# A feature-interaction tower on one core: contractions joined and moved, the split of the next chunk ahead of its border, and one tile of seven of the first chunk as one f32 product

## The reference, cut to what matters

```python
e = jnp.stack([tbl_f[ids[:, f]] for f in range(39)], axis=1)        # B=512, M=39, D=16
x0 = xk = e
for W in (W0, W1):                                                 # H = 128 and 128
    Wr = W.reshape(39, xk.shape[1], 128)
    xk = jnp.einsum('bid,bjd,ijh->bhd', x0, xk, Wr)
    outs.append(xk)
z = jnp.sum(jnp.concatenate(outs, axis=1), axis=-1)                # (512, 256)
h = jnp.concatenate([z, dense_ctx], axis=1)
h = jnp.maximum(h @ W_top1 + b_top1, 0.0)
h = jnp.maximum(h @ W_top2 + b_top2, 0.0)
y = h @ W_top3                                                     # (512, 1)
```

## Time and profile before

| what | us |
|---|---|
| runs, median of 3 | 365.79 |
| the profiled execution | 365.56 |
| its span in the profile | 363.8 |
| TensorE (matmul) busy | 229.9 (63%) |
| VectorE busy | 164.8 (45%) |
| ScalarE busy | 158.9 (44%) |
| GpSimd busy | 98.0 (27%) |

### The profile page before, as it was taken

One profiled execution on the slowest core, in us unless ns is written; L12 is line 12 of the kernel. 1 busy time (PEld: TensorE's weight loads), 2 busy tenths in 40 slices (PEclk: granted clock), 3 DMA queues, 4 the chain that ended last, 5 costly groups with the idle time before them and its releaser, 6 DMA issues.

```text
span 363.8 us, 4707 instructions
## 1 busy us (share of the span) xinstructions
PE 229.9 (63%) x1673; PEld 176.2 (48%) x1673; DVE 164.8 (45%) x333; ACT 158.9 (44%) x307; POOL 98.0 (27%) x107
## 2 busy tenths in 40 slices
PE   5311100010001001889998999989999999999997
PEld 4200000000000000746765887667688877788896
DVE  4440000000000100589897867979784867745411
ACT  4600000000000300488887757986856877666411
POOL 5777777777777730000000000000000000000000
PEclk9655555555555555699999999999999999999999
DMA  6800100000000000019100000000000000000000
GB/s 175 253 14 6 10 6 6 7 7 6 6 7 6 6 5 0 0 31 304 46 21 2 1 2 1 2 0 3 1 2 2 0 3 0 3 0 2 0 2 0
DMA packets 7834, 8.61 MB, mean 24 GB/s; under 512 B 2759, under 2 KB 5420, under 8 KB 7812
## 3 DMA queue, kind: packets, MB, share of 16 engines
q1 hardware_dynamic: 4516, 7.48, 7.2%
q0 software_dynamic: 3296, 0.85, 2.5%
HBM read 8.32 MB, written 0.00 MB: 23 GB/s over the span
## 4 chain that ended last, share of the span: by engine, by line
PE 48%; issue 35%; DVE 7%; ACT 7%; another core or an unknown queue 2%; DMA 1%; ACTq 0%; DVEq 0%
PE turn_bank L542 10%; PE g_bank L512 5%; PE pair_bank L455 5%; PE x_bank L479 5%; PE x_bank L482 4%; PE x_bank L481 4%; DVE onehot L791 3%; ACT prod_hi L1027 2%; DVE prod_lo L864 2%; PE x_bank L522 2%; PE turn_bank L580 2%; PE g_bank L706 2%; PE turn_bank L553 1%; ACT prod L1022 1%
## 5 line engine op out<-in xcount | busy, mean ns | idle before, releaser
L430 POOL DMA_INDIRECT emb<-tbl,ids_sb x103 | 97.8, 950 | 33.5 <-issue 31.1
L1022 ACT ACTIVATE prod<-pair_bank 128x512 f32<-128x512 f32 (+1 forms) x112 | 66.2, 600 | 43.0 <-PE pair_bank L455 38.7
L864 DVE TENSOR_TENSOR prod_lo<-prod,prod_hi 128x512 fp32r<-128x512 f32 x96 | 65.1, 686 | 2.6
L479 PE MATMUL x_bank<-prod_hi,pair_w_hi 128*128 128x512 f32 (+1 forms) x112 | 63.4, 566 | 2.0 <-DVE prod_lo L864 1.9
L1142 ACT ACTIVATE looked<-pair_bank 128x192 f32<-128x192 f32 x2 | 0.6, 328 | 104.4 <-remote 104.4
L808 DVE COPY_PREDICATED looked<-odd,pair_bank 128x192 f32<-128x192 int32 x2 | 0.6, 370 | 97.6 <-issue 97.6
L455 PE MATMUL pair_bank<-x,sel 117*128 117x512 bf16 (+1 forms) x112 | 42.8, 384 | 0.9 <-ACT x L1004 0.7
L542 PE MATMUL turn_bank<-g_sb,w_sb 128*128 128x128 f32 x312 | 42.3, 279 | 0.0
L542 PEld LDWEIGHTS turn_bank<-g_sb,w_sb 128*128 128x128 f32 x312 | 39.4, 192 | 3.0 <-issue 1.2
L1027 ACT ACTIVATE prod_hi<-prod 128x512 fp32r<-128x512 f32 x64 | 40.0, 625 | 0.1
L482 PE MATMUL x_bank<-prod_hi,pair_w_lo 128*128 128x512 f32 x96 | 38.1, 397 | 0.0
(11 more groups left out here) (143 smaller groups left out, 315.2 us busy)
## 6 DMA issues: line engine op xcount, KB each, us to landing
emb<-tbl,ids_sb POOLq DMA_INDIRECT x103
tab<-small SPq DMA_DIRECT2D x2, 560.0 KB
wt<-w_top SPq DMA_DIRECT2D x2, 512.0 KB, 4.4
tab<-small SPq DMA_DIRECT2D x1, 504.0 KB
wa<-pair_w_a SPq DMA_DIRECT2D x1, 448.0 KB
wb<-pair_w_b SPq DMA_DIRECT2D x1, 448.0 KB
wtd<-w_dense SPq DMA_DIRECT2D x1, 256.0 KB
dense_sb<-dense_t SPq DMA_DIRECT2D x1, 256.0 KB
```

The source lines that it names most:

```text
L430: pool.indirect_dma_start(out=emb[:, at:at + D], out_offset=None, in_=tables[f], in_offset=bass.IndirectOffsetOnAxis(ap=ids_sb[:, c * M + ...
L479: mm = pe.matmul(x1_banks[k % 2][:, :], pair_w_hi[p, t, :], hi(n), start=(t == 0), stop=(t == FULL))
L864: dve.tensor_tensor(lo(n), prod[rows, n % RING, :], prod_hi[rows, n % RING2, :], ALU.subtract).then_inc(lo_done, 1)
L1022: act.activation(prod[0:ROWS[t], n % RING, :], pair_bank[n % 2][0:ROWS[t], :], ACT.Square).then_inc(sq_done, 1)
```

## The change

- `contract_d(k, 0)` and `(k, 1)` stand together in one step (`G_AT = 4`), at the second tile of the block after next. The second half's G goes to free columns of `misc_bank` and of `x1_banks[k % 2]`. The four copies follow one step later (`G_KEPT = 2`). `turn_x` moves from a block's first tile to its fifth, `spread_x` from the third to the sixth.
- `look_up_later` runs as one piece of twenty products at a block's fifth tile, into the two G banks; its copies and picks become two of half the size. Chunks 2 and 3 are looked up one block later. The second part of the ids is spread at tile 17 instead of 10, and `later_ids` holds 24 slots, of which the first 4 are used twice.
- The seam goes; all borders have one form. The next chunk's splits stand at tiles 1, 2 and 6 of block 3 for chunk 1, and at tiles 0, 1, 3 and 4 for chunks 2 and 3. The turns and the copies to `x3` stand at the end of block 3's last step, ahead of two tiles of layer 1. Chunk 0's layer 2 runs in blocks 2 and 3 of chunk 1 like the others.
- Tile 3 of each of the four blocks of chunk 0 (`whole(n)`) is neither rounded nor subtracted: ScalarE squares it into free columns of `emb`, and layer 1 takes it as one f32 product with an f32 weight tile.
- `keep_x1h` on ScalarE stands between the square and the rounding of its step.

```diff
+WHOLE_AT = 3
...
-SEAMS = (1,)
-SPLIT_AT = (4, 6)
+SPLIT_AT = ((), ((1, 2), (6, 6)), ((0, 1), (3, 4)), ((0, 1), (3, 4)))
...
-G_AT = (3, 6)
+G_AT = 4
+G_KEPT = 2
+XT_AT = 4
+SPREAD_AT = 5
...
-LATE_AT = (NT + 1, NT + 3)
+LATE_AT = (NT + 1, 2 * NT + 3)
+IDS_HELD = 24
+LOOK_AT = 4
...
+        prod_whole = emb[:, 0:COLS]
...
+        def look_step(c, part):
+            return ((c - 1) * NB + part + (c > 1 and PARTS[c] < 3)) * NT + LOOK_AT
+        def look_at(n):
...
+        def hot_at(n):
+            return [(c, part, r) for c in range(1, NCH) for part in range(PARTS[c]) for r in range(HOT)
+                    if max(look_step(c, part) - 6 + r, (c - 1) * NB * NT) == n]
...
+        def later_cols(f):
+            return g_bank[f // 2][:, f % 2 * 2 * E:(f % 2 + 1) * 2 * E]
+        def later_rows(half, row):
+            return looked_rows(g_bank[half], 2, row)
...
+        def whole(n):
+            return n < NB * NT and n % NT == WHOLE_AT
+        def split_tiles(n):
+            return n - sum(whole(m) for m in range(n))
...
+            if pair == 1:
+                return x1_banks[k % 2][:, 0:2 * QC] if half else misc_bank[:, QC:3 * QC]
...
+                kept = 2 * (c * NB - 2)
+                if c and part == 0:
+                    pe.wait_ge(g_dve, kept)
+                if c and part == 1:
+                    pe.wait_ge(g_act, kept)
...
+                wait(pe, g_act, 2 * (k - 1))
...
-                pe.wait_ge(lo_done, n + 1)
+                if whole(n):
+                    pe.wait_ge(sq_done, n + 1)
+                    pe.matmul(x1_banks[k % 2][:, :], pair_w_whole[:, :], prod_whole, start=False,
+                              stop=False).then_inc(l1_done, 1)
+                    return
+                pe.wait_ge(lo_done, split_tiles(n + 1))
                 if t == 0:
                     wait(pe, x1_done, k - 1)
+                    wait(pe, g_dve, 2 * (k - 1))
                     if k == 1:
                         pe.wait_ge(dense_act, 2)
-                    c, j = divmod(k, NB)
...
+                if k == K - 1:
+                    pe.wait_ge(g_dve, 2 * k)
...
-                    pe.wait_ge(xblk_done, k + 1)
-                if k == K - 1 and pair == 1:
+                    pe.wait_ge(xblk_done, min(k + 2, K))
+                    pe.wait_ge(picked, len(SETS) + looks_ahead_of((k + 2) * NT))
+                    wait(pe, g_act, 2 * k)
+                    wait(pe, g_dve, 2 * k)
+                elif k == K - 1:
                     pe.wait_ge(x1_done, K + 1)
-                else:
-                    wait(pe, g_act, 2 * k + pair)
-                    wait(pe, g_dve, 2 * k + pair)
...
-            def look_up_later(c, part, r0, r1):
-                for r in range(r0, r1):
+            def look_up_later(c, part):
+                pe.wait_ge(picked, len(SETS) + nth(c, part))
+                pe.wait_ge(dense_dve, 2)
+                k = look_step(c, part) // NT
+                kept = 2 * (k - 1)
+                wait(pe, g_act, kept)
+                wait(pe, g_dve, kept)
+                for r in range(HOT):
                     pe.wait_ge(later_hot_done, HOT * nth(c, part) + r + 1)
                     for f in range(LATER):
                         rows = tab_parts[part // 2][:, LATER * (part % 2) + f, 2 * r:2 * r + 2, :, :]
-                        mm = pe.matmul(later_bank(part)[:, f * 2 * E:(f + 1) * 2 * E], later_hot[:, r, f, :],
-                                       rows.rearrange("p r q d -> p (r q d)"), start=(r == 0 and f == 0),
-                                       stop=(r == HOT - 1 and f == LATER - 1))
+                        mm = pe.matmul(later_cols(f), later_hot[:, r, f, :],
+                                       rows.rearrange("p r q d -> p (r q d)"), start=(r == 0 and f % 2 == 0),
+                                       stop=(r == HOT - 1 and f % 2 == 1))
                     mm.then_inc(later_row, 1)
...
-            def seam(c):
...
                 if late and t == 0:
                     layer1(m)
                     layer1(m + 1)
-                    pe.wait_ge(x1_done, n // NT - 1)
-                    turn(c, 0)
-                    pe.wait_ge(xblk_done, n // NT)
-                    turn(c, 1)
-                    pe.wait_ge(sq_done, n - 1)
-                    turn(c, 2)
-                    layer1(m + 2)
                 if n < TILES:
                     select_pair(n)
                 if m >= 0 and (not late or t >= LAG1):
                     layer1(m)
-                if late and t == 1:
-                    layer1(m + 2)
-                if t == 0 and n < TILES:
+                if late and t in (1, 2):
+                    layer1(m + 1)
+                if c + 1 < NCH and j == NB - 1 and t == NT - 1:
+                    pe.wait_ge(x1_done, n // NT)
+                    turn(c + 1, 0)
+                    pe.wait_ge(xblk_done, n // NT + 1)
+                    turn(c + 1, 1)
+                    pe.wait_ge(sq_done, n)
+                    turn(c + 1, 2)
+                if t == XT_AT and n < TILES:
                     turn_x(n // NT)
-                if u == 0 and k >= 1 and not ended(k - 1):
+                for part in look_at(n):
+                    look_up_later(*part)
+                if u == 0 and k >= 1:
                     turn_x1(k - 1)
-                if u in G_AT and k >= 1 and not ended(k - 1):
-                    contract_d(k - 1, G_AT.index(u))
+                if u == G_AT and k >= 1:
+                    contract_d(k - 1, 0)
+                    contract_d(k - 1, 1)
                 if n >= TILES:
                     return
...
             def take_lo(n):
+                if whole(n):
+                    return
                 k, t = divmod(n, NT)
                 if t in DVE_ROUNDS:
-                    dve.wait_ge(hi_dve, len(DVE_ROUNDS) * k + DVE_TO[t + 1])
+                    dve.wait_ge(hi_dve, len(DVE_ROUNDS) * k + DVE_TO[t + 1] - sum(whole(m) for m in range(n)))
                 else:
...
-                seam = c in SEAMS and j == 0
                 if c >= 1 and j == 0 and t == 0:
-                    keep_turned(c)
-                    if seam:
-                        keep_g(k - 1, 1)
-                    else:
-                        take_lo(n - 1)
+                    take_lo(n - 1)
                 tile(n)
-                if 1 <= j <= looks and t == 2:
-                    pick_later(c + 1, j - 1)
-                if t == 2:
-                    spread_x(k)
-                if t == 1 and k >= 2 and not ended(k - 1) and not ended(k - 2):
+                for part in look_at(n - 1):
+                    pick_later(*part)
+                if t == G_KEPT and k >= 2:
                     keep_g(k - 2, 0)
+                    keep_g(k - 2, 1)
                 if j == 0 and c >= 2 and t == 4:
                     relu1(c - 2)
-                if t == 4 and k >= 2 and not ended(k - 1) and not ended(k - 2):
-                    keep_g(k - 2, 1)
-                if j < looks and t >= 2:
-                    later_one_hot(c + 1, j, t - 2)
-                if looks and j == looks and t == 3:
+                if t == SPREAD_AT:
+                    spread_x(k)
+                for part in hot_at(n):
+                    later_one_hot(*part)
+                if look_at(n - 2) and look_at(n - 2)[0][1] == looks - 1:
                     words(0, c + 1)
-                for p in range(len(SPLIT_AT) - 1):
-                    if splits and t == SPLIT_AT[p]:
+                if splits and t == NT - 1:
+                    take_lo(n - 1)
+                for p in range(len(CUTS) - 1):
+                    if splits and t == SPLIT_AT[c + 1][p][0]:
                         split_rest(c + 1, CUTS[p], CUTS[p + 1])
-                    if splits and t == SPLIT_AT[p] + 1:
+                    if splits and t == SPLIT_AT[c + 1][p][1]:
                         split_lo(c + 1, CUTS[p], CUTS[p + 1])
                 if splits and t == NT - 1:
-                    take_lo(n - 1)
-                    if c + 1 in SEAMS:
-                        take_lo(n)
-                        keep_g(k - 1, 0)
-                        keep_g(k - 1, 1)
-                    split_rest(c + 1, *CUTS[-2:])
-                    split_lo(c + 1, *CUTS[-2:])
-                    if c + 1 in SEAMS:
-                        keep_g(k, 0)
+                    keep_turned(c + 1)
...
+            dve.tensor_scalar(pair_w_whole[:, :], pair_w[:, WHOLE_AT, :], 0.5, None, ALU.mult)
...
                 act.wait_ge(pair_sel, n + 1)
-                wait(act, lo_done, n + 1 - RING)
+                if whole(n):
+                    wait(act, l1_done, n + 1 - NT)
+                    act.activation(prod_whole, pair_bank[n % 2][:, :], ACT.Square).then_inc(sq_done, 1)
+                    return
+                wait(act, lo_done, split_tiles(n + 1 - RING))
...
+                for part in look_at(n - 1):
+                    keep_looked_later(*part)
```

(30 more changed lines are left out.)

95 lines of the change are left out of this document (29 added, 66 removed).

## The result

The changed kernel took 361.94 us (median of 4 runs, 361.16 to 362.48) beside 365.6 us for the kernel before: ratio 0.9884 [0.9866, 0.9901], so 3.6 to 4.9 us less (the two medians themselves are 3.7 apart). Forecast were 359.0, range 354.8 to 363.6: the sign and the range hold, the size doesn't. The sum said -6.8 us; over the part of the program that the change touches, -4.0 came. The profiled execution took 362.48.

The account below looks back on a forecast made before the run. TensorE was taken to set the pace, busy 9.30 of 9.36 us in a block with a look-up. The terms summed to -6.8 us, from 365.79 to 359.0 us on the median's scale, range 354.8 to 363.6.

Parts of the forecast that it names:

- contractions joined: At L512, a block's two contraction groups side by side save 0.31 us in nine blocks, 0.40 in six: -5.2 us.
- f32 products: One tile of seven, four times, costs 0.86 us instead of 0.705 for three products: +0.6 us; VectorE's relief counts 0.
- look-ups: Four look-ups no longer wait for the copy of the turned x1: -0.9 us.
- border to chunk 1: Losses of 3.7 us against 2.3 today, ScalarE's splits standing in a short block: +1.4 us, bounds -2.3 and +4.
- x1h first, other blocks: ScalarE copies x1 before rounding, so TensorE waits less for x1h, but G copies stand ahead: net -0.3 us.
- Late next: ScalarE: At the border to chunk 1, ScalarE has 9.7 us of work in a block of 8.1 us TensorE time.
- New waits of TensorE: Waits for kept G ahead of turn of x, look-up and layer 1 are met by copies one to two steps before.
- A: Rival: joining the contractions saves nothing, the entry being paid at each pair or hidden; -1.6 us, 364.2; 5%.
- C: Rival: ScalarE isn't late at all at the border to chunk 1; 3.7 us better, 355.3; 13%.
- B: Rival: border to chunk 1 costs more, or the f32 product its upper price; +3 to +4 us, 362.5; 12%.
- E: Rival: the change does nothing, the waits only move; 366 us; 4%.
- D: Rival: ScalarE paces every block, G copies ahead of x1h costing 0.75 us in all fifteen; +4.2 us, 370; 8%.

Follow-up runs that it names:

- the unjoined kernel: Changed kernel with a block's two contractions apart again, the first ahead of the step's layer 1, the second behind it: 367.72 us, ratio 1.0042.
- the early splits: Changed kernel with chunk 1's splits at tiles 0, 1, 3 and 4 of block 3 instead of 1, 2 and 6: 230.18 us, ratio 0.9821.
- later turns: Changed kernel with the turn of x1 one step later in blocks 3, 4, 8 and 12, its copy too in the last three: 232.64 us, ratio 0.9914.
- first and third set of runs: Two of three sets, each on one chip; the kernel before took 365.99 us in the first, 365.36 in the third, 234.38 in the second.

## Why the prediction was right in sign and off in size

Against the terms of its sum (us, before to after, from record end to record end, a wait or an entry being what a record takes beyond its usual time):

| term | forecast | measured |
|---|---|---|
| contractions joined | -5.2 | -4.5 |
| f32 products | +0.6 | +0.7 |
| look-ups | -0.9 | -1.4 |
| second spread | -0.7 | -0.7 |
| borders to chunks 2 and 3 | -2.15 | -2.25 |
| last block | +0.45 | +0.55 |
| border to chunk 1 | +1.4 | +1.9 |
| x1h first, other blocks | -0.3 | +0.4 |
| new waits of first products | 0 | +1.0 |
| new waits of the small network | 0 | +0.3 |
| sum | -6.8 | -4.0 |

**Joined contractions: right cause, 0.7 too large.** The step that failed is "Joining saves 0.85-0.54 = 0.31 in nine blocks and 0.94-0.54 = 0.40 in the six that have layer 2 behind". The fifteen entries came as read, 0.20 each, 3.0 in all. (contract_d lost 3.89, but 0.76 of that is the seam's wait for the copy of the turned x1; the unjoined kernel, which has the entries and not that wait, shows the 3.0.) The exits gave 1.5 instead of 2.2. The 0.40 counts a dear exit, into layer 2 (0.196 in both kernels), as gone in six blocks. Of those there were seven and there still are six: in chunk 1 two joined groups that had a selection behind now have layer 2. What went were mostly cheap exits, into selections and look-ups (0.10 each). The unjoined kernel lost more, 5.6, since all its second exits go into a product of layer 1 (0.195).

**The f32 product** came at the price forecast, two records 0.43 apart. That VectorE's relief is worth nothing held only where no chain over VectorE ends in a wait of TensorE; at the border to chunk 1 one did.

**Spread, borders to chunks 2 and 3, last block** came as stated. The look-ups gained 0.5 more: the wait in front of them was worth its 0.9, and the rest comes from fewer changes between their products and others, as one piece of twenty stands where there were three (going from them into layer 2 costs 0.07). Their 1.65 in the table by function holds 0.5 more, the exits out of contractions that are counted with the joining here.

**Border to chunk 1: the place right, the reason wrong.** The forecast waits of x1h (1.25) and of the turn (1.5) were 0.95 and 1.97, the two behind the border (0.35 and 0.5) were 0.39 and 0.65; all losses there are 3.95 against 2.05 in the kernel before (forecast 3.7 against 2.3). The step that failed is "Late next: ScalarE": the sum of its work (9.7 in 8.1 us) was taken for the cause, and the early splits do the same work with 1.35 us less lost. At the turn the cause was that the small split stood last, behind VectorE's two subtractions, which the walk named, and all else in both queues; its shares are not told apart.

**x1h first and the first products: the terms that were missing.** "New waits of TensorE (kept G ahead of turn of x, look-up and layer 1) are met" failed, and nothing was put down for the rounding that now stands behind x1h on ScalarE. First products wait 0.33 to 0.38 us at four places (records that end at 170.2, 188.7, 206.4 and 210.4), 1.4 in all, less 0.3 won in the first block. At 188.7 and 210.4 the product starts right behind VectorE's copy of G, a wait that the change has added; with early splits, where that copy comes later, the same place costs 1.0 us and the profile names it (`g_sb` L902). At 170.2 and 206.4 it waits for `prod_lo`. With x1h behind the rounding again the waits at 206.4 and 210.4 go and those at 170.2 and 188.7 stay, so the new order has made the former two alone. It also makes mlp2 wait twice, 0.15 each. The turns of x1 of the first blocks of chunks 2 and 3 lose 0.36 each, against 0.2 to 0.3 forecast, five others 0.05, and the three waits of the kernel before were worth the 0.6 stated. These three rows of the table are 2.0 of the 2.8 us by which the sum missed; joining and the border to chunk 1 missed by 0.7 and 0.5 and the look-ups made up 0.5.

Of the rivals, A fell by the unjoined kernel; C's premise, nothing late at that border, isn't met, and the early splits win 1.35 of its 3.7; B's border cost 0.5 us more than forecast and not 3 to 4, E falls with the interval, and D's place is real (waits for x1h) at 0.36 us in a few blocks instead of 0.75 in fifteen.

## What to carry to other kernels

Put groups of partial-array matmuls side by side before polishing anything else: here fifteen fewer entries and exits were worth all of the gain and more (4.5 of work against a net 4.0). When a late engine shows at a border, walk the chain through every engine's queue and move its first link before concluding that the engine has too much to do; the sum of its work doesn't tell the one from the other. When a copy becomes the condition of a product that didn't need it before, walk the copying engine's queue too. And an edit that relieves an engine off the path is worth what the next wait behind it is worth: measure it again after that wait is gone, since the sign can turn.

## What was not expected of the hardware

**A wait and the clock.** TensorE waited 2.56 us in the kernel without f32 products and 2.26 us in the one with later turns, each time behind a stretch at full clock, and the granted clock then stood at 0.50 (1.2 GHz) for 3.4 us of the profile, though TensorE was busy throughout. Behind the waits of 1.97 us (changed kernel; 1.89 to 1.98 in four further profiles) and 2.18 (f32 product at tile 4) it stayed at 2.4 GHz. These are too few for more than this: a wait of that size cost some 1.6 us beyond itself in both kernels.

**The head and the chip.** In the first and third set of runs TensorE issues a matmul only every 2 to 3 us in most of the 150 us of the head. By stretch, the kernel before in its first profile, then the one with early splits on the other chip:

```profile
20.00:60.00 40.00, 4.30 (x18) 1.77 (x17) 2.42 (x5) 0.00 (x0) 30.25 (x33) 0.50 0.08 9
60.00:140.00 80.00, 6.93 (x29) 3.05 (x29) 1.22 (x4) 2.76 (x4) 54.45 (x58) 0.50 0.07 6
```

```profile
20.00:60.00 40.00, 36.98 (x269) 25.04 (x267) 35.68 (x82) 35.41 (x74) 30.70 (x31) 1.00 0.39 99
60.00:140.00 80.00, 78.81 (x606) 61.79 (x605) 63.67 (x132) 58.93 (x124) 62.63 (x58) 1.00 0.08 7
```

GpSimd issues its gathers at the same rate in both (33 and 31, then 58). On the one chip TensorE issues 18 and 29 matmuls meanwhile, each after an idle time that nothing in the profile explains; on the other 269 and 606, and the whole program is over 130 us earlier. Half clock alone doesn't do it: on the other chip TensorE got through more than twice the matmuls in a stretch at half clock too (the kernel before, then the one with early splits):

```profile
10.30:17.10 6.80, 3.05 (x30) 2.42 (x30) 3.23 (x5) 4.74 (x3) 5.05 (x6) 0.58 0.96 291
```

```profile
10.30:17.10 6.80, 5.59 (x69) 5.43 (x70) 5.43 (x13) 6.69 (x7) 4.98 (x6) 0.50 1.02 291
```

(The profile of the unjoined kernel gives a mean granted clock of 1.000 for the whole span. It is no evidence here: its clock records start only at 152.65 us, and its matmuls of the head take what the kernel before's take at half clock, 6.91 us for 29 against 6.93.) The cause wasn't tried and stays open. The changed kernel itself was not run on that chip; the one with early splits was 4.2 us under the kernel before there.
